# Second aggregation of a graph network: one exp per edge weight, and the sum of weights partly formed on VectorE

## The chip, the cores and the metric

One core of one Trainium2 chip runs the whole program in one launch. The metric is the device time of that launch in microseconds (us), lower is better.

## The reference, cut to what matters

Two graph attention networks follow each other on 1250 nodes and 21250 edges (20000 given, and one loop per node). The change lies in the first layer of the second network: 4 heads of 512 channels each. For a head with node scores a_s (source) and a_d (destination):

```
e(s, d)  = leaky_relu(a_s[s] + a_d[d], 0.2)            for every edge s -> d
p(s, d)  = exp(e(s, d) - max over the edges into d)
out[d]   = sum over s of p(s, d) * h[s]  /  (sum over s of p(s, d) + 1e-16)  + b
h        = elu(out)
```

## The kernel before, in words

The kernel treats the graph as a dense matrix: CT[s, d] counts the edges from s to d (125 rows of sources by 10 tiles of sources by 1250 destinations). Its last stages are `project_layer1`, which computes h and the scores, `aggregate_layer1` (L1489), which is the formula above, `project_out_layer1` and `aggregate_last`. Stages are separated by a barrier of all engines.

`aggregate_layer1` runs over 4 heads, per head over 3 pieces of the destinations (418, 416 and 416 columns, called thirds), per third over 10 tiles of 125 sources: 12 thirds, 120 steps. In the code g is the step, n the third (`ENDS` is 12), s the source tile, i the head.

In one step ScalarE (`act`) computes two exponentials of a 125x416 tile, since leaky_relu(x) is max(x, 0.2x): exp(u + a) and exp(v + 0.2a), where u and v are rows that depend on the destination and a is the score of the source, a column of one value per partition (`col_src`, L1641). VectorE (`dve`) takes the larger of the two (L1696), bounds it by 1 and multiplies it with CT (L1698). That is the weight p. ScalarE rounds p to the format that TensorE takes (`p_hi`, L1611), VectorE subtracts to get the rest (`p_lo`, L1688). TensorE (`pe`) then runs 14 products of 416 columns: for each of the four chunks of 128 channels three (h_hi p_hi, h_hi p_lo, h_lo p_hi; L1755), and two of p_hi and p_lo with a matrix of ones (L1735), which give the sum of the weights, the same in all 128 rows. They stand ahead of the step's other products, in step 0 behind them.

A third fills five banks of PSUM: four chunks and the sums. There are eight, so the next third reuses banks: its chunk 3 needs the bank of chunk 0 of the third before (`bank_is_free`, waiting for `left`), its sums that of chunk 1.

The end of a third is done inside the next third, at hand-placed steps. At s = 3 VectorE copies the sums out of PSUM (`invert`, L1665), takes the reciprocal (L1667) and multiplies chunks 0 and 1 by it (`leave`, L1676), at s = 4 chunks 2 and 3. ScalarE does the exponential of the elu for one chunk in each of s = 4 to 7, three instructions each (`elu_exp`, L1623, L1625, L1627), and VectorE finishes one chunk in each of s = 6 to 9 (`elu`, L1683). SyncE (`sp`) stores each finished chunk.

Every engine takes its instructions in the order of the code. In step g ScalarE issues the two exponentials of g and then rounds p of g-1; VectorE issues maximum and product of g and then the rest of p of g-1. Buffers of e, p_hi and p_lo go round in a ring of six (`RING`), so ScalarE's rounding of step g waits until TensorE has used step g-6 (`p_used`).

`col_src` is written once, in `project_layer1` (`spread_scores`, L1367 and L1368).

Of the kernel before, what the change touches and what calls it, by code (L numbers as in the profile page):

```python
# [4 lines left out]
F32 = mybir.dt.float32  # L5
F32R = mybir.dt.float32r
# [4 lines left out]
ALU = mybir.AluOpType  # L11
ACT = mybir.ActivationFunctionType
# [5 lines left out]
T = 125  # L18
NT = N // T
# [1133 lines left out]
def project_layer1(nc, core, xT, x2_rows, w, wa, h_rows, score_rows, col_src, u_col, v_col):  # L1153
# [13 lines left out]
    with ExitStack() as ctx:  # L1167
# [182 lines left out]
        def _(dve):  # L1350
# [13 lines left out]

            def spread_scores():
                dve.wait_ge(score_kept, NT)
                v.tensor_copy(col_src[0][:, 0:heads, :], score[:, 0])  # L1367
                v.tensor_scalar(col_src[1][:, 0:heads, :], score[:, 0], SLOPE, None, ALU.mult)  # L1368

            def maximum(m):  # L1370
# [118 lines left out]
def aggregate_layer1(nc, core, h_rows, col_src, bias, turned_rows, w_next):  # L1489


    CT = core.CT
    THIRDS = [(0, 418), (418, 416), (834, 416)]
    W = THIRD
# [2 lines left out]
    STEPS_ALL = H1 * STEPS  # L1497
    ENDS = 3 * H1
    RING = 6
    PER = CW + 1  # L1500
    with ExitStack() as ctx:
        sb, pb, sem = core.tools(ctx)
        uv_other = sb("uv", [T, 2, N], F32)
        uv = (first_uv_of_layer1(core), uv_other[:])
        h = sb("h_parts", [T, NT, 2, C1], F32)
        e = sb("e", [T, RING, 2, W], F32)
        p_hi = sb("p_hi", [T, RING, W], F32R)
        p_lo = sb("p_lo", [T, RING, W], F32R)
        ones_f = sb("ones_f", [T, 128], F32)
# [9 lines left out]
        bias_in = sem("bias_in")  # L1519
        ones_set = sem("ones_set")  # L1520
        exp_ready = sem("exp_ready")
        more_ready = sem("more_ready")
        p_ready = sem("p_ready")
        p_hi_ready = sem("p_hi_ready")
        p_split = sem("p_split")
# [18 lines left out]
        def bank(n, c):  # L1544
            return (n * PER + c) % 8

# [9 lines left out]
        @block.sync  # L1556
        def _(sp):
            def load_third(i, t3):
                a, w = THIRDS[t3]
                if i >= 2:  # L1560
                    sp.wait_ge(exp_ready, (i - 2) * STEPS + (t3 + 1) * NT)
                for kind in range(2):
                    dma_in_two(sp, uv[i % 2][:, kind, a:a + w],
                               core.uv_rows[kind, i * NT:(i + 1) * NT, :].rearrange("(o t) p -> o (t p)", o=1)[:, a:a + w]
                               .broadcast_to([T, w]), uv_in[i % 2][t3])

            def load_h(i, s):
                if i:
                    sp.wait_ge(p_used, (i - 1) * STEPS + 2 * NT + s + 1)
                dma_in_two(sp, h[:, s], h_rows[i, s * T:(s + 1) * T], h_loaded[s])  # L1570

            def store(n, c):
                i, t3 = divmod(n, 3)
                a, w = THIRDS[t3]
                sp.wait_ge(out_ready, n * CW + c + 1)
                sp.dma_start(turned_rows[i * CW + c, :, a:a + w], out_f[:, n % 2, c, 0:w]).then_inc(stored[n % 2][c], 16)

            sp.dma_start(b_col[:], bias).then_inc(bias_in, 16)
            for stored_h in core.h1_stored:
                sp.wait_ge(stored_h, 64 * (UNITS - 1))  # L1580
            for s in range(NT):
                load_h(0, s)
            for n in range(ENDS):
                i, t3 = divmod(n, 3)
                if i + 1 < H1:
                    load_third(i + 1, t3)
                stores = [c for c in range(CW) if n]
                if n == ENDS - 4:
                    sp.wait_ge(core.h1_stored[1], 64 * UNITS)
                    sp.wait_ge(core.h1_late, 64)  # L1590
                for s in range(NT):
                    if t3 == 2 and i + 1 < H1:
                        load_h(i + 1, s)
                    if s >= 2 and stores:
                        store(n - 1, stores.pop(0))
            sp.dma_start(core.w_first[:], w_next[0].rearrange("(k p) c -> p k c", p=128)[:, 0:K1 // 2, :]).then_inc(core.w_first_in, 16)
            for s in range(2):
                for c in range(CW):
                    sp.wait_ge(stored[s][c], 16 * (ENDS // 4))
            for t in range(2):  # L1600
                sp.dma_start(core.f_raw[:, t], turned_rows[0:K1 // 2, :, t * T:(t + 1) * T].rearrange("k p n -> p k n")).then_inc(core.f_first_in, 16)

        @block.scalar
        def _(act):
            a = nc.scalar
            def round_p(g):
                w = THIRDS[g // NT % 3][1]
                act.wait_ge(p_ready, g + 1)
                if g >= RING:
                    act.wait_ge(p_used, g - RING + 1)  # L1610
                a.activation(p_hi[:, g % RING, 0:w], e[:, g % RING, 0, 0:w], ACT.Copy).then_inc(p_hi_ready, 1)  # L1611

            def elu_exp(n, c):
                i, t3 = divmod(n, 3)
# [14 lines left out]
            for g in range(STEPS_ALL):  # L1629
                n, s = divmod(g, NT)  # L1630
                i, t3 = divmod(n, 3)
                at, w = THIRDS[t3]
                if s == 0:
                    if i == 0:
                        act.wait_ge(core.first_uv_in, 64)
                    else:
                        act.wait_ge(uv_in[i % 2][t3], 64 * ((i + 1) // 2))
                if g >= RING:
                    act.wait_ge(p_split, g - RING + 1)
                for kind in range(2):  # L1640
                    last = a.activation(e[:, g % RING, kind, 0:w], uv[i % 2][:, kind, at:at + w], ACT.Exp,  # L1641
                                        bias=col_src[kind][:, i, s:s + 1])
                last.then_inc(exp_ready, 1)
                if g == 0:
                    act.wait_ge(ones_set, 1)
                    a.activation(ones[:], ones_f[:], ACT.Copy).then_inc(ones_set, 1)
                if g:
                    round_p(g - 1)
                if g == 3:
                    act.wait_ge(bias_in, 16)  # L1650
                    a.activation(b_minus[:], b_col[:], ACT.Copy, scale=-1.0).then_inc(bias_in, 16)
                    act.wait_ge(bias_in, 32)
                if n and 4 <= s < 8:
                    elu_exp(n - 1, s - 4)
            round_p(STEPS_ALL - 1)

        @block.vector
        def _(dve):
# [2 lines left out]

            def invert(n):
                w = THIRDS[n % 3][1]
                dve.wait_ge(summed, n + 1)
                v.tensor_scalar(sums[:, 0, 0:w], p_o[:, bank(n, CW), 0:w], 1e-16, None, ALU.add).then_inc(sum_kept, 1)  # L1665
                dve.wait_ge(sum_kept, n + 1)
                v.reciprocal(sums[:, 1, 0:w], sums[:, 0, 0:w]).then_inc(inverted, 1)  # L1667
                dve.wait_ge(inverted, n + 1)
# [16 lines left out]
            def rest_of_p(g):  # L1685
                w = THIRDS[g // NT % 3][1]
                dve.wait_ge(p_hi_ready, g + 1)
                v.tensor_tensor(p_lo[:, g % RING, 0:w], e[:, g % RING, 0, 0:w], p_hi[:, g % RING, 0:w].bitcast(F32),  # L1688
                                ALU.subtract).then_inc(p_split, 1)

            for g in range(STEPS_ALL):
                n, s = divmod(g, NT)
                at, w = THIRDS[n % 3]
                low = e[:, g % RING, 0, 0:w]
                dve.wait_ge(exp_ready, g + 1)
                v.tensor_tensor(low, low, e[:, g % RING, 1, 0:w], ALU.max).then_inc(more_ready, 1)  # L1696
                dve.wait_ge(more_ready, g + 1)
                v.scalar_tensor_tensor(low, low, 1.0, CT[:, s, at:at + w], ALU.min, ALU.mult).then_inc(p_ready, 1)  # L1698
                if g:
                    rest_of_p(g - 1)  # L1700
                if n and s == 3:
                    invert(n - 1)
                    leave(n - 1, 0)
                    leave(n - 1, 1)
                if n and s == 4:
                    leave(n - 1, 2)
                    leave(n - 1, 3)
                if n and 6 <= s:
                    elu(n - 1, s - 6)
# [6 lines left out]
        def _(pe):  # L1716
# [10 lines left out]
                        pe.wait_ge(sum_kept, m + 1)  # L1727

            def sum_weights(g, n, s, w):
                if g == 0:  # L1730
                    pe.wait_ge(ones_set, 2)
                if s == 0:
                    bank_is_free(n, CW)
                for pp in (p_hi, p_lo):
                    last = nc.tensor.matmul(p_o[:, bank(n, CW), 0:w], ones[:], pp[:, g % RING, 0:w],  # L1735
                                            start=(s == 0 and pp is p_hi), stop=(s == NT - 1 and pp is p_lo))
                if s == NT - 1:
                    last.then_inc(summed, 1)
                return last

            for g in range(STEPS_ALL):
                n, s = divmod(g, NT)
# [2 lines left out]
                if t3 == 0:  # L1745
                    pe.wait_ge(h_loaded[s], 32 * (i + 1))
                pe.wait_ge(p_split, g + 1)
                if s:
                    sum_weights(g, n, s, w)
                for c in range(CW):  # L1750
                    if s == 0:
# [4 lines left out]
                                                start=(s == 0 and j == 0), stop=(s == NT - 1 and j == 2))  # L1756
                    if s == NT - 1 and c < CW - 1:
                        last.then_inc(chunk_done, 1)
                if s == 0:
                    last = sum_weights(g, n, s, w)  # L1760
                last.then_inc(p_used, 1)
            pe.wait_ge(left, (ENDS - 1) * CW)
            keep_busy(nc, core.ident, p_o[:, bank(ENDS - 2, CW - 1), 0:128], 14)
# [917 lines left out]
```

## Time and profile before

| | us |
|---|---|
| median of 3 runs | 1923.69 (1923.25 to 1928.69) |
| the profiled execution, its own time | 1930.16 |
| its span, first to last instruction | 1928.4 |
| TensorE busy / VectorE busy / ScalarE busy | 1839.7 / 1443.6 / 1030.9 |
| `aggregate_layer1`: first product to last | 1273.6 to 1609.5 |

The profile shows one execution. Durations are of single instructions; since an engine can start an instruction while the one before it finishes, the distance from start to start can be shorter than a duration. A time in square brackets at the end of a timeline row is the idle time of the engine before it, and what ended it. Matmuls are pipelined, so their durations overlap by about half.

### The profile page before, as it was taken

What the parts mean: (1) busy time and instruction counts of PE and PEld (TensorE: products, weight loads), DVE (VectorE), ACT (ScalarE), POOL (GpSimd) and SP (SyncE); (2) the same over time, 40 slices, a digit from 0 to 9 for tenths busy, and PEclk for the clock granted to TensorE, in tenths of its full rate; (3) what the DMA queues carried; (4) which work ended last, traced back from release to release, by engine and by line L of the source; (5) the groups of instructions that cost most, each with busy time, mean ns of one, the idle gap of its engine ahead of it and who ended that gap; (6) DMA issues with size and microseconds to landing.
All of it is one profiled execution on the core that took longest, in us unless ns stands there. A gap on an engine that the chain in (4) does not pass through costs nothing. (4 is left out here: it accounts for less than half of the span.)

```text
span 1928.4 us, 30682 instructions
## 1 busy us (share of the span) xinstructions
PE 1839.7 (95%) x11399; PEld 1776.6 (92%) x11399; DVE 1443.6 (75%) x2468; ACT 1030.9 (53%) x1634; POOL 142.1 (7%) x139
## 2 busy tenths in 40 slices
PE   7999999998999999998999999989999998999998
PEld 5877699998999999988999999989999998999997
DVE  8888599998888988965465549457888886346766
ACT  4676412218898889864211322257778875232632
POOL 5100211201000000000111011100000000000000
PEclk9999999999999999999999999989999999999989
DMA  4221335355455436619644466462342406544302
GB/s 126 67 64 54 99 103 149 101 133 142 134 111 131 108 77 149 145 16 248 185 141 143 135 208 188 141 193 79 108 143 66 138 28 204 156 129 126 99 9 80
DMA packets 179273, 234.12 MB, mean 121 GB/s; under 512 B 75943, under 2 KB 151655, under 8 KB 178889
## 3 DMA queue, kind: packets, MB, share of 16 engines
q1 hardware_dynamic: 170407, 202.98, 38.5%
q0 software_dynamic: 7984, 27.24, 4.9%
q10 hardware_dynamic: 748, 2.10, 0.4%
q8 instruction: 86, 1.41, 0.3%
q14 instruction: 48, 0.39, 0.1%
HBM read 167.27 MB, written 65.00 MB: 120 GB/s over the span
## 5 line engine op out<-in xcount | busy, mean ns | idle before, releaser
L1755 PE MATMUL p_o<-p_hi,h_parts 125*128 125x416 f32 (+1 forms) x960 | 283.0, 356 | 7.4 <-DVE z L1676 6.1
L1138 PE MATMUL p_o<-first_room,p 125*125 125x193 f32 x1200 | 202.2, 329 | 6.2 <-ACT res L1020 2.9
L1138 PEld LDWEIGHTS p_o<-first_room,p 125*125 125x125 f32 x1200 | 197.1, 189 | 8.0 <-issue 6.7
L1138 PE MATMUL p_o<-h_in,p 125*125 125x193 f32 x1200 | 200.9, 330 | 3.6 <-ACT res L1020 3.6
L1138 PEld LDWEIGHTS p_o<-h_in,p 125*125 125x125 f32 x1200 | 198.7, 190 | 5.0 <-issue 3.8
L1755 PEld LDWEIGHTS p_o<-p_hi,h_parts 125*128 125x128 f32 x960 | 182.0, 190 | 13.7 <-DVE z L1676 10.1
L781 DVE CUSTOM_DVE_ANT_0 max_junk<-src_row,G 125x1250 bf16<-125x1250 f32 x120 | 184.8, 1612 | 3.6 <-ACT src_row L819 1.5
L885 PE MATMUL p_h<-pw_hi,x1T 128*125 128x384 f32 x720 | 187.3, 341 | 0.0
L1088 DVE TENSOR_TENSOR e<-e 125x1250 f32<-125x1250 f32 x120 | 174.3, 1453 | 17.2 <-ACT e L1050 17.1
L1474 PE MATMUL p_h<-pw_hi,x2T 128*125 128x256 f32 (+1 forms) x960 | 177.8, 287 | 3.9 <-DVE h_out L1430 3.9
L1093 DVE SCALAR_TENSOR_TENSOR p<-e,CT 125x1250 f32<-125x1250 f32 x120 | 175.3, 1461 | 5.7 <-PE p_o L1138 1.7
L1755 PE MATMUL p_o<-p_lo,h_parts 125*128 125x416 f32 (+1 forms) x480 | 169.9, 354 | 0.0
L1050 ACT ACTIVATE e<-first_room,col 125x1250 f32<-125x1250 f32 x120 | 151.1, 1344 | 6.9 <-DVE p L1093 5.5
L1474 PEld LDWEIGHTS p_h<-pw_hi,x2T 128*125 128x125 f32 x960 | 150.4, 190 | 4.2 <-DVE h_out L1430 4.1
L1050 ACT ACTIVATE e<-uv,col 125x1250 f32<-125x1250 f32 x120 | 149.0, 1349 | 1.2 <-DVE p L1093 1.2
L1474 PE MATMUL p_h<-pw_lo,x2T 128*125 128x256 f32 (+1 forms) x480 | 136.9, 285 | 0.0
L885 PEld LDWEIGHTS p_h<-pw_hi,x1T 128*125 128x125 f32 x720 | 131.7, 188 | 1.2 <-issue 1.2
L2012 PE MATMUL p_y<-fw_hi,f_hi 128*125 128x384 f32 x360 | 121.9, 339 | 4.2 <-DVE fw_lo L1935 4.1
L885 PE MATMUL p_h<-pw_lo,x1T 128*125 128x384 f32 x360 | 122.5, 340 | 0.0
L2012 PE MATMUL p_y<-fw_lo,f_hi 128*125 128x384 f32 x360 | 121.6, 338 | 0.0
L2012 PE MATMUL p_y<-fw_hi,f_lo 128*125 128x384 f32 x360 | 121.5, 337 | 0.0
L481 PE MATMUL p_count<-src_hot,dst_hot 125*125 125x416 bf16 (+1 forms) x588 | 112.7, 350 | 6.3 <-DVE dst_hot L286 6.3
(285 smaller groups left out, 3839.3 us busy)
## 6 DMA issues: line engine op xcount, KB each, us to landing
f_raw<-turned SPq DMA_DIRECT2D x40, 500.0 KB, 8.8
h_parts<-h_rows SPq DMA_DIRECT2D x40, 448.0 KB
turned<-tail_room SPq DMA_DIRECT2D x18, 625.0 KB, 6.9
G<-turned SPq DMA_DIRECT2D x20, 562.5 KB
h_rows<-tail_room SPq DMA_DIRECT2D x22, 424.4 KB
h_rows<-h_out SPq DMA_DIRECT2D x16, 560.0 KB
h_rows<-tail_room SPq DMA_DIRECT2D x14, 560.0 KB
first_room<-in_w_gat POOLq DMA_DIRECT2D x36, 192.0 KB, 2.7
```

The lines of the kernel that those rows point to most:

```text
L481: last = nc.tensor.matmul(p_count[:, i, 0:w], dst_hot[:, h, :], src_hot[:, h, a:a + w], start=False, stop=False, skip_group_check=True)
L781: v.tensor_tensor_reduce(out=junk[:, t % 2, :], in0=src_row[:, h % 2, :], in1=G[:, t, :], scale=1.0, scalar=NO_EDGE, op0=ALU.subtract, op1 ...
L885: last = nc.tensor.matmul(p_h[:, (u * NT + t) % 4, 0:width], xp[:, k, at], wp[:, u, k, :], start=(k == 0 and n == 0), stop=(k == KD - 1 an ...
L1050: last = a.activation(e[:, g % RING, kind, :], uv[hh][:, kind, :], ACT.Exp, bias=col_src[kind][:, bass.ds(i * 2 + hh, 1), s])
L1088: v.tensor_tensor(e[:, g % RING, 0, :], e[:, g % RING, 0, :], e[:, g % RING, 1, :], ALU.max).then_inc(more_ready, 1)
L1093: v.scalar_tensor_tensor(p[:, g % RING, :], e[:, g % RING, 0, :], 1.0, CT[:, s, :], ALU.min, ALU.mult).then_inc(p_ready, 1)
L1138: last = nc.tensor.matmul(p_o[:, b, n * 256:n * 256 + C0 + 1], p[:, g % RING, d * T:(d + 1) * T], h_in[hh][:, s, 0:C0 + 1], start=(s == 0 ...
L1474: last = nc.tensor.matmul(p_h[:, n % 4, 0:width], xp[:, k, at], wp[:, q % 2, k, 0:width], start=(k == 0 and j == 0), stop=(k == KD - 1 and ...
L1755: last = nc.tensor.matmul(p_o[:, bank(n, c), 0:w], h[:, s, kind, cols].bitcast(F32R), pp[:, g % RING, 0:w], start=(s == 0 and j == 0), sto ...
L2012: last = nc.tensor.matmul(p_y[:, t % 2, half, 0:CW], fp[:, n % 2, kk, :], wp[:, k, cols], start=(k == 0 and j == 0), stop=(k == KO - 1 and ...
```

## The change

Three things, all in `aggregate_layer1`, and one line in `project_layer1`.

1. Since exp is monotone, the larger is taken first: VectorE computes max(u + 0.8a, v) in one instruction two steps ahead (`larger_exponent`, `AHEAD` = 2), and ScalarE takes one exp of it, with 0.2a as bias. `col_src[0]` now holds 0.8a.
2. The weights of source tiles 0 to 3 are added on VectorE (`add`, three instructions per third), the sum is rounded (`acc_hi`, ScalarE) and its rest taken (`acc_lo`, VectorE), and TensorE multiplies these two with ones in step 6 instead of the eight products with ones of steps 0 to 3.
3. The copy of the sums out of PSUM moves from VectorE to ScalarE (`keep_sums`), which issues it in s = 3 behind the rounding.

```
 def spread_scores():
-    v.tensor_copy(col_src[0][:, 0:heads, :], score[:, 0])
+    v.tensor_scalar(col_src[0][:, 0:heads, :], score[:, 0], 1 - SLOPE, None, ALU.mult)

 # load_third (SyncE)
-    sp.wait_ge(exp_ready, (i - 2) * STEPS + (t3 + 1) * NT)
+    sp.wait_ge(larger, (i - 2) * STEPS + (t3 + 1) * NT)

 # ScalarE
+def keep_sums(n):
+    act.wait_ge(summed, n + 1)
+    if n:
+        act.wait_ge(inverted, n)
+    a.activation(sums[:, 0, 0:w], p_o[:, bank(n, CW), 0:w], ACT.Copy, bias=1e-16).then_inc(sum_kept, 1)
 for g in range(STEPS_ALL):
-    if g >= RING:
-        act.wait_ge(p_split, g - RING + 1)
-    for kind in range(2):
-        last = a.activation(e[:, g % RING, kind, 0:w], uv[i % 2][:, kind, at:at + w], ACT.Exp,
-                            bias=col_src[kind][:, i, s:s + 1])
-    last.then_inc(exp_ready, 1)
+    act.wait_ge(larger, g + 1)
+    a.activation(e[:, g % RING, 0:w], e[:, g % RING, 0:w], ACT.Exp, bias=col_src[1][:, i, s:s + 1]).then_inc(exp_ready, 1)
     if g:
         round_p(g - 1)
+    if s == ADDED:
+        act.wait_ge(added, (n + 1) * (ADDED - 1))
+        if n:
+            act.wait_ge(p_used, (n - 1) * NT + SUM_AT + 1)
+        a.activation(acc_hi[:, 0:w], acc[:, 0:w], ACT.Copy).then_inc(acc_hi_ready, 1)
+    if n and s == 3:
+        keep_sums(n - 1)
     if n and 4 <= s < 8:
         elu_exp(n - 1, s - 4)
 round_p(STEPS_ALL - 1)
+keep_sums(ENDS - 1)

 # VectorE
 def invert(n):
-    dve.wait_ge(summed, n + 1)
-    v.tensor_scalar(sums[:, 0, 0:w], p_o[:, bank(n, CW), 0:w], 1e-16, None, ALU.add).then_inc(sum_kept, 1)
     dve.wait_ge(sum_kept, n + 1)
     v.reciprocal(sums[:, 1, 0:w], sums[:, 0, 0:w]).then_inc(inverted, 1)
+def larger_exponent(g):
+    if s == 0:
...
+    if g >= RING:
+        dve.wait_ge(p_split, g - RING + 1)
+    v.scalar_tensor_tensor(e[:, g % RING, 0:w], uv[i % 2][:, 0, at:at + w], col_src[0][:, i, s:s + 1],
+                           uv[i % 2][:, 1, at:at + w], ALU.add, ALU.max).then_inc(larger, 1)
+def add(g):
...
+    dve.wait_ge(p_ready, g + 1)
+    v.tensor_tensor(acc[:, 0:w], before, e[:, g % RING, 0:w], ALU.add).then_inc(added, 1)
+def rest_of_sum(n):
+    dve.wait_ge(acc_hi_ready, n + 1)
+    v.tensor_tensor(acc_lo[:, 0:w], acc[:, 0:w], acc_hi[:, 0:w].bitcast(F32), ALU.subtract).then_inc(acc_split, 1)
+for g in range(AHEAD):
+    larger_exponent(g)
 for g in range(STEPS_ALL):
     dve.wait_ge(exp_ready, g + 1)
-    v.tensor_tensor(low, low, e[:, g % RING, 1, 0:w], ALU.max).then_inc(more_ready, 1)
-    dve.wait_ge(more_ready, g + 1)
     v.scalar_tensor_tensor(low, low, 1.0, CT[:, s, at:at + w], ALU.min, ALU.mult).then_inc(p_ready, 1)
+    if g + AHEAD < STEPS_ALL:
+        larger_exponent(g + AHEAD)
     if g:
         rest_of_p(g - 1)
+    if 0 < s < ADDED:
+        add(g)
+    if s == ADDED + 1:
+        rest_of_sum(n)
     if n and s == 3:
         invert(n - 1)
         leave(n - 1, 0)

 # TensorE
 def sum_weights(g, n, s, w):
-    if s == 0:
+    if s == ADDED:
         bank_is_free(n, CW)
+    passing = [p_hi[:, g % RING, 0:w], p_lo[:, g % RING, 0:w]]
+    if s == SUM_AT:
+        pe.wait_ge(acc_split, n + 1)
+        passing += [acc_hi[:, 0:w], acc_lo[:, 0:w]]
+    for k, pp in enumerate(passing):
+        last = nc.tensor.matmul(p_o[:, bank(n, CW), 0:w], ones[:], pp,
+                                start=(s == ADDED and k == 0), stop=(s == NT - 1 and k == 1))
...
-    if s:
+    if s >= ADDED:
         sum_weights(g, n, s, w)
...
-    if s == 0:
-        last = sum_weights(g, n, s, w)
```

`ADDED` is 4 and `SUM_AT` is 6. The ring of e holds one tile per step instead of two.

## Rows read from the trace of the kernel before

**Rows 1.** Busy time by stretch: window, length, PE, PEld, DVE, ACT, POOL, clock, DMA.

```profile
1385.00:1413.00 28.00, 27.44 (x144) 26.78 (x143) 24.28 (x42) 22.79 (x44) 0.00 (x0) 1.00 0.15 48
```

**Rows 2.** Who waited for whom, 1270 to 1625: us in total, times, longest.

```profile
ACT tail_room L1623 <- DVE z L1676: 45.2, 11, 6.5
DVE e L1696 <- ACT e L1641: 39.2, 39, 1.4
...
PEld p_o L1755 <- DVE z L1676: 10.1, 11, 1.0
DVE sums L1665 <- PE p_o L1735: 9.9, 2, 5.4
```

**Rows 3.** Timeline of VectorE in one third: start, duration, line, operation, idle before.

```profile
1388.32 2.77 DVE L1667 RECIPROCAL sums<-sums 128x418 f32<-128x418 f32 x1
...
1404.31 0.59 DVE L1696 TENSOR_TENSOR e<-e 125x416 f32<-125x416 f32 x1 [0.93 <-ACT e L1641]
1404.94 0.59 DVE L1698 SCALAR_TENSOR_TENSOR e<-e,CT 125x416 f32<-125x416 f32 x1
1405.45 0.58 DVE L1688 TENSOR_TENSOR p_lo<-e,p_hi 125x416 fp32r<-125x416 f32 x1
1405.95 0.65 DVE L1683 SCALAR_TENSOR_TENSOR tail_room<-z,b_col,tail_room 128x418 f32<-128x418 f32 x1
1406.52 0.58 DVE L1696 TENSOR_TENSOR e<-e 125x416 f32<-125x416 f32 x1
...
1415.85 2.75 DVE L1667 RECIPROCAL sums<-sums 128x416 f32<-128x416 f32 x1
```

**Rows 4.** Timeline of ScalarE in the same third.

```profile
1391.75 0.65 ACT L1623 ACTIVATE tail_room<-z,b_minus 128x418 f32<-128x418 f32 x1 [3.88 <-DVE z L1676]
...
1393.47 1.16 ACT L1641 ACTIVATE e<-uv,col 125x416 f32<-125x416 f32 x2
1394.54 0.54 ACT L1611 ACTIVATE p_hi<-e 125x416 fp32r<-125x416 f32 x1
1394.98 0.63 ACT L1623 ACTIVATE tail_room<-z,b_minus 128x418 f32<-128x418 f32 x1
```

**Rows 5.** Timeline of TensorE in the same third.

```profile
1384.00 0.35 PE L1735 MATMUL p_o<-p_hi,ones 125*128 125x418 f32 x1
...
1386.67 0.35 PE L1735 MATMUL p_o<-p_hi,ones 125*128 125x418 f32 x1
...
1391.77 0.46 PE L1755 MATMUL p_o<-p_hi,h_parts 125*128 125x416 f32 x1 [0.56 <-DVE z L1676]
```

**Rows 6.** Groups of VectorE by line and shape: busy us, mean ns, idle before.

```profile
L1698 DVE SCALAR_TENSOR_TENSOR e<-e,CT 125x416 f32<-125x416 f32 x80 | 47.4, 593 | 2.8
...
L1688 DVE TENSOR_TENSOR p_lo<-e,p_hi 125x416 fp32r<-125x416 f32 x80 | 46.9, 586 | 1.2 <-ACT p_hi L1611 1.2
...
L1683 DVE SCALAR_TENSOR_TENSOR tail_room<-z,b_col,tail_room 128x416 f32<-128x416 f32 x28 | 18.1, 646 | 0.0
```

**Rows 7.** ScalarE's copy of 384 columns out of PSUM, in another stage.

```profile
L846 ACT ACTIVATE tail_room<-p_h x60: 491/493/497, 245.4 to 431.9; 125x384 f32<-125x384 f32 x60
```

**Rows 8.** VectorE timeline: the first reciprocal, the last two, the start of the next stage.

```profile
1305.71 2.77 DVE L1667 RECIPROCAL sums<-sums 128x418 f32<-128x418 f32 x1
...
1581.06 2.75 DVE L1667 RECIPROCAL sums<-sums 128x416 f32<-128x416 f32 x1
...
1607.42 0.59 DVE L1665 TENSOR_SCALAR sums<-p_o 128x416 f32<-128x416 f32 x1 [5.42 <-PE p_o L1735]
1608.05 2.75 DVE L1667 RECIPROCAL sums<-sums 128x416 f32<-128x416 f32 x1
...
1613.87 0.18 DVE L2185 CAST fw_hi<-wa 128x32 fp32r<-128x32 f32 x1 [0.94 <-PEq L70]
```

**Rows 9.** TensorE timeline: the product behind the first third's wait for h.

```profile
1280.43 0.71 PE L1735 MATMUL p_o<-p_hi,ones 125*128 125x418 f32 x1 [3.85 <-DMA h_parts<-h_rows]
```

**Rows 10.** The small instruction of `spread_scores`.

```profile
L1367 DVE COPY col<-score x1: 174/174/174, 1111.4 to 1111.4; 125x40 f32<-125x40 f32 x1
```

More of the change, by code:

```diff
@@ L1499, in aggregate_layer1 @@
     RING = 6
+    AHEAD = 2
+    ADDED = 4
+    SUM_AT = ADDED + 2
     PER = CW + 1
@@ L1505, in aggregate_layer1 @@
         h = sb("h_parts", [T, NT, 2, C1], F32)
-        e = sb("e", [T, RING, 2, W], F32)
+        e = sb("e", [T, RING, W], F32)
+        acc = sb("acc", [T, W], F32)
+        acc_hi = sb("acc_hi", [T, W], F32R)
+        acc_lo = sb("acc_lo", [T, W], F32R)
         p_hi = sb("p_hi", [T, RING, W], F32R)
@@ L1521, in aggregate_layer1 @@
         exp_ready = sem("exp_ready")
-        more_ready = sem("more_ready")
+        larger = sem("larger")
+        added = sem("added")
+        acc_hi_ready = sem("acc_hi_ready")
+        acc_split = sem("acc_split")
         p_ready = sem("p_ready")
@@ L1610, in round_p @@
                     act.wait_ge(p_used, g - RING + 1)
-                a.activation(p_hi[:, g % RING, 0:w], e[:, g % RING, 0, 0:w], ACT.Copy).then_inc(p_hi_ready, 1)
+                a.activation(p_hi[:, g % RING, 0:w], e[:, g % RING, 0:w], ACT.Copy).then_inc(p_hi_ready, 1)
+            def keep_sums(n):
+                w = THIRDS[n % 3][1]
+                act.wait_ge(summed, n + 1)
+                if n:
+                    act.wait_ge(inverted, n)
+                a.activation(sums[:, 0, 0:w], p_o[:, bank(n, CW), 0:w], ACT.Copy, bias=1e-16).then_inc(sum_kept, 1)
             def elu_exp(n, c):
@@ L1632, in _ @@
                 at, w = THIRDS[t3]
-                if s == 0:
[L1634 to L1637, printed above, removed]
-                if g >= RING:
-                    act.wait_ge(p_split, g - RING + 1)
-                for kind in range(2):
-                    last = a.activation(e[:, g % RING, kind, 0:w], uv[i % 2][:, kind, at:at + w], ACT.Exp,
-                                        bias=col_src[kind][:, i, s:s + 1])
-                last.then_inc(exp_ready, 1)
+                act.wait_ge(larger, g + 1)
+                a.activation(e[:, g % RING, 0:w], e[:, g % RING, 0:w], ACT.Exp, bias=col_src[1][:, i, s:s + 1]).then_inc(exp_ready, 1)
                 if g == 0:
@@ L1687, in rest_of_p @@
                 dve.wait_ge(p_hi_ready, g + 1)
-                v.tensor_tensor(p_lo[:, g % RING, 0:w], e[:, g % RING, 0, 0:w], p_hi[:, g % RING, 0:w].bitcast(F32),
+                v.tensor_tensor(p_lo[:, g % RING, 0:w], e[:, g % RING, 0:w], p_hi[:, g % RING, 0:w].bitcast(F32),
                                 ALU.subtract).then_inc(p_split, 1)
+            def larger_exponent(g):
+                n, s = divmod(g, NT)
+                i, t3 = divmod(n, 3)
+                at, w = THIRDS[t3]
+                if s == 0:
+                    if i == 0:
+                        dve.wait_ge(core.first_uv_in, 64)
+                    else:
+                        dve.wait_ge(uv_in[i % 2][t3], 64 * ((i + 1) // 2))
+                if g >= RING:
[3 more added lines that the diff above has]
+            def add(g):
+                n, s = divmod(g, NT)
+                w = THIRDS[n % 3][1]
+                if s == 1:
+                    if n:
+                        dve.wait_ge(acc_split, n)
+                    before = e[:, (g - 1) % RING, 0:w]
+                else:
+                    dve.wait_ge(added, n * (ADDED - 1) + s - 1)
+                    before = acc[:, 0:w]
+                dve.wait_ge(p_ready, g + 1)
+                v.tensor_tensor(acc[:, 0:w], before, e[:, g % RING, 0:w], ALU.add).then_inc(added, 1)
+            def rest_of_sum(n):
+                w = THIRDS[n % 3][1]
+                dve.wait_ge(acc_hi_ready, n + 1)
+                v.tensor_tensor(acc_lo[:, 0:w], acc[:, 0:w], acc_hi[:, 0:w].bitcast(F32), ALU.subtract).then_inc(acc_split, 1)
+            for g in range(AHEAD):
+                larger_exponent(g)
             for g in range(STEPS_ALL):
@@ L1693, in _ @@
                 at, w = THIRDS[n % 3]
-                low = e[:, g % RING, 0, 0:w]
+                low = e[:, g % RING, 0:w]
                 dve.wait_ge(exp_ready, g + 1)
-                v.tensor_tensor(low, low, e[:, g % RING, 1, 0:w], ALU.max).then_inc(more_ready, 1)
-                dve.wait_ge(more_ready, g + 1)
                 v.scalar_tensor_tensor(low, low, 1.0, CT[:, s, at:at + w], ALU.min, ALU.mult).then_inc(p_ready, 1)
+                if g + AHEAD < STEPS_ALL:
+                    larger_exponent(g + AHEAD)
                 if g:
                     rest_of_p(g - 1)
+                if 0 < s < ADDED:
+                    add(g)
+                if s == ADDED + 1:
+                    rest_of_sum(n)
                 if n and s == 3:
@@ L1729, in sum_weights @@
             def sum_weights(g, n, s, w):
-                if g == 0:
+                if g == ADDED:
                     pe.wait_ge(ones_set, 2)
-                if s == 0:
+                if s == ADDED:
                     bank_is_free(n, CW)
-                for pp in (p_hi, p_lo):
-                    last = nc.tensor.matmul(p_o[:, bank(n, CW), 0:w], ones[:], pp[:, g % RING, 0:w],
-                                            start=(s == 0 and pp is p_hi), stop=(s == NT - 1 and pp is p_lo))
+                passing = [p_hi[:, g % RING, 0:w], p_lo[:, g % RING, 0:w]]
[5 more added lines that the diff above has]
+                                            start=(s == ADDED and k == 0), stop=(s == NT - 1 and k == 1))
                 if s == NT - 1:
                     last.then_inc(summed, 1)
-                return last
             for g in range(STEPS_ALL):
@@ L1758, in _ @@
                         last.then_inc(chunk_done, 1)
-                if s == 0:
-                    last = sum_weights(g, n, s, w)
                 last.then_inc(p_used, 1)
```

## The prediction

> **What bounds the kernel now.** I read the busy times by stretch first, then the waits, then the timelines of VectorE, ScalarE and TensorE over one third. In 28 us in the middle of the stage TensorE is busy for 27.44, VectorE for 24.28, ScalarE for 22.79, at full clock [rows 1]. By the busy shares alone TensorE would be the bound. The waits say otherwise: in 12 thirds VectorE waits for TensorE only twice, and for ScalarE's exponentials 39 times, 39.2 us in all; TensorE waits once in each of eleven thirds for z, the chunk that VectorE must take out before its bank is free, 10.1 us in all [rows 2]. An engine that nobody waits for in the steady thirds, and that itself waits once in each, has slack. TensorE's slot is (1386.67 - 1384.00) / 14 = 0.1907 us per product [rows 5], so its 140 products of a third take 26.7 us. The third takes (1581.06 - 1305.71) / 10 = 27.54 us, reciprocal to reciprocal [rows 8].
>
> What makes 27.54 is a chain through VectorE and ScalarE, and it closes from rows. From the reciprocal at 1388.32, z of chunk 0 is there when ScalarE starts the elu at 1391.75, 3.43 us later [rows 3, 4]. ScalarE then has, in order, four elus of 1.72 (1391.75 to 1393.47), and between them three times a pair of exps (1.07) and a rounding (0.44) [rows 4]: 6.86 + 4.53. Behind the fourth elu it gives the exp pair of step 8, 1.16 long, and VectorE, idle until then, starts 0.03 later. Sum 3.43 + 6.86 + 4.53 + 1.19 = 16.01; the row stands at 1404.31 - 1388.32 = 15.99 [rows 3]. From there VectorE never idles: steps 8 and 9 and steps 0 to 3 of the next third at 0.63 + 0.51 + 0.50 = 1.64 from start to start, two elus of 0.57, and the copy of the sums, 0.62: 9.8 + 1.1 + 0.6 = 11.5, against 1415.85 - 1404.31 = 11.54 [rows 3]. Total 27.53.
>
> **The change, part by part.**
>
> One exp instead of two. ScalarE's pair of 1.07 becomes one of 0.53, 0.63 long (half the pair's slot, and 1.16 less that) [rows 4]. Four of them lie in the chain: 2.12 us per third come off it. The other six lie where ScalarE waits for VectorE, and bring nothing.
>
> The larger taken first. The maximum (0.63 from start to start, because the product behind it needs its result) goes, and an addition and maximum with a column operand comes. It has a twin in the trace: the elu's last instruction, the same two operations with a column, 646 ns long, 0.57 from start to start, against 0.51 for the product without a column [rows 3, 6]. It depends on nothing just ahead of it, being two steps early. A step on VectorE is then 0.51 + 0.56 + 0.505 = 1.575, 0.06 less than before. What the trace does not show is one such instruction right behind the product. Its start is bounded from below by the 0.51 that any independent successor gets, from above by the 0.63 of a dependent one [rows 3]. I take 0.51, since it is independent, and keep 0.63 for a rival. ScalarE waits for it, but step g's is issued one full step ahead of its use.
>
> The sum of four tiles. VectorE gets three additions and one subtraction per third, 0.505 each from start to start (the slot between 1405.45 and 1405.95, same form) [rows 3]. The additions stand in steps 1 to 3, inside the chain: +1.52. The subtraction stands in step 5, where VectorE goes on to wait for ScalarE's exp: covered. ScalarE's rounding of the sum, 0.54 like the other rounding, stands at s = 4 ahead of the first elu, where ScalarE sits idle for 3.88 us during the reciprocal [rows 4]; were that cover gone it would add 0.45.
>
> TensorE loses eight products with ones and gets two: 6 fewer per third, 134 x 0.1907 = 25.55 us. It waits for the rest of the sum in step 6, many microseconds after step 5 on VectorE. I expect no stall.
>
> The copy of the sums on ScalarE. VectorE's 0.62 leaves the chain. ScalarE takes some 0.52: 384 columns take 493 ns [rows 7], and 32 more at most 0.03 more; below, nothing reasonable under 0.49. Behind its wait for TensorE are queued exp 4, the rounding of 3, the rounding of the sum and the first elu, about 1.4 us of work that fits in the reciprocal's 2.8. It is a new hop, TensorE to ScalarE to VectorE, worth 0.03 as the other hops.
>
> Nothing changes for the queues of SyncE and GpSimd: no DMA is added or moved, and the one wait of SyncE that is renamed comes true earlier. The multiplication in `spread_scores` replaces a 0.17 us copy in another stage, where it is one of hundreds of small instructions [rows 10]: nothing.
>
> **The sum for a steady third.** 3.43 + 6.86 + 3 x (0.53 + 0.44) + 0.63 + 0.03 = 13.86 to the start of step 8's product; then six steps of 1.575, two elus of 0.565 and three additions of 0.505: 9.45 + 1.13 + 1.52 = 12.10. Total 25.96, 1.58 less. Can TensorE follow? From the reciprocal its chunk 3 begins 3.45 later [rows 3, 5]; up to the end of step 9's ones there are 3 + 36 + 70 + 2 + 2 = 113 products, 112 x 0.1907 + 0.35 for the last, 0.04 to wake ScalarE, 0.52 + 0.03 for the copy: 25.75. The same sum with 119 products gives 26.34 for the last third of before, where the row shows 1607.42 - 1581.06 = 26.36 [rows 8]. So TensorE's loop is 0.2 shorter than the other, which keeps the say.
>
> The ends. In the first third TensorE sets the pace and waits for h to land, until 1280.43 [rows 9]; what it saves before that is lost. Behind it are four fewer products up to the sums: 0.8. In the last third VectorE waits for TensorE (5.42) [rows 8]: six fewer products, 1.1. The stage ends with the same reciprocal and four multiplications, and the next begins at the barrier [rows 8], so its work moves forward whole.
>
> Together 10 x 1.58 + 0.8 + 1.1 = 17.7 us. The profiled execution took 1930.16 at a span of 1928.4; it would give 1912.5 at 1910.7. It lies 6.5 above the median of 1923.69, in work the change does not touch, so the median becomes **1906.0**.
>
> **The rivals.**
>
> TensorE sets the pace (0.13). If one of ScalarE's or VectorE's slots is a little shorter than I take it, the third falls to the 25.75 of TensorE's loop: 17.9 + 1.9, 1903.9. For it speaks that only 0.2 us lie between the loops; against it, that the same slots reproduced 27.54 to 0.01.
>
> The instruction with a column does not overlap with the product ahead of it (0.12). Then 0.11 more in each of six steps of the chain, 26.6: 9.2 + 1.9, 1912.6. No pair of this form stands in the trace.
>
> VectorE becomes the bound outright, and the kernel slower (0.03). The place is the start of each VectorE instruction: today it begins 0.08 before the one ahead ends (0.50 between starts at 0.58 long) [rows 3]. If in the new order, where every instruction carries a wait and an increment for another engine, they ran end to end, a third would be 10 x (0.593 + 0.646 + 0.586) + 8 x 0.586 + 4 x 0.646 + 2.75 = 28.3 [rows 6, 3]. This is 0.8 above 27.54, ten times, less 1.9: 1929.4. It turns slower than before once a third passes 27.7, that is 1.8 above my sum. Against it: the subtraction at 1405.45 and the elu behind it carry both and overlap. The Trainium skill (VectorE: DVE Perf Modes, Terms) says that each VectorE instruction is followed by a drain and the next cannot issue until the pipe is empty; by that rule this case would be the likely one. The trace does not agree, with 0.50 between the starts of instructions of 0.58.
>
> Something behind the stage gives part back (0.04). The following stage's first inputs are loaded by SyncE during the last third; if they came late, a few microseconds would return, 1910 or so. Both the stores ahead of them and the stage's end move forward together, so I see no reason.
>
> **How the numbers follow.** The forecast has 0.68. Its own uncertainty is 0.3 us per third, 3 us in all, and the runs of before reach 5.0 above their median, which gives 1902.5 to 1911.5; this takes in the first rival and stops just short of the second. A measurement tells about 0.3% (5.8 us) from nothing. Faster by more, below 1917.9: the forecast, both close rivals, and most of the rest, 0.94. Within: 0.03, a mixture of the last two. Slower: 0.03.
>
> **What would show it right or wrong.** Reciprocals 25.96 apart (25.75 and no idle of VectorE ahead of the products if TensorE leads; 26.6 if the column instruction is dear); the new instruction's mean near 646 ns and 0.56 to its successor; VectorE waiting for exps in steps 7 and 8 only, about 0.5 each; VectorE's reciprocal following the last addition with no idle; 1608 products in place of 1680, and TensorE's wait for z down from about 0.9 to 0.4 per third. I am wrong in the mechanism if TensorE waits for `p_lo` within a third, or if the third shrinks by something other than the exps.

## The result, and the profile after

The changed kernel takes 1907.91 us (median of 4 runs, 1905.64 to 1911.14) against 1925.05 for the kernel before beside it (4 runs), a ratio of 0.9909 with a 95% interval of 0.9891 to 0.9927: about 17 us less. The forecast was 1906.0 from 1923.69, 17.7 less. A second measurement, with the experiments, gave 0.9921 (0.9907 to 0.9934), about 15 us less. One execution of an experiment took 4993.24 us and one of the kernel before, beside it, 6732.26: the figures below leave both out.

The profiled execution has a span of 1903.9 us. That is 24.5 less than the profiled one of before, more than the medians show, and the stages say where the rest lies. Taken from TensorE's first instruction of `aggregate_layer1` to VectorE's first of the next stage, the stage fell by 19.76 us (345.22 to 325.46); what is ahead of it took 3.84 less in this execution and what follows 0.90 less. Behind the stage the change touches nothing, and ahead of it only the small instruction of [rows 10]; over the fourteen profiled executions of this study the stage began anywhere from 1263.16 to 1271.65, whatever the kernel.

The busy times by stretch of the changed kernel, the same 28 us as in [rows 1], with the same columns:

```profile
1385.00:1413.00 28.00, 27.81 (x148) 27.18 (x147) 27.04 (x48) 20.27 (x39) 0.00 (x0) 1.00 0.28 81
```

Here the reader sees the exchange: VectorE went from 24.28 to 27.04 of 28, ScalarE from 22.79 to 20.27, and TensorE runs 148 products where it ran 144.

Who waited for whom in the changed kernel, 1270 to 1600 (us in total, times, longest), answering to [rows 2]:

```profile
ACT sums L1629 <- PE p_o L1793: 36.6, 12, 8.6
ACT p_hi L1622 <- DVE e L1746: 33.0, 44, 0.9
ACT tail_room L1641 <- DVE z L1691: 23.6, 11, 2.2
DVE sums L1682 <- ACT sums L1629: 12.7, 2, 8.2
DVE e L1746 <- ACT e L1652: 10.1, 22, 0.5
...
PEld p_o L1812 <- DVE z L1691: 5.5, 11, 0.6
```

VectorE's waits for exps went from 39, 39.2 us in all, to 22 of about 0.46 each, two per third. TensorE's waits for z halved, 10.1 to 5.5. VectorE waits for the sums only twice, in the first third and the last: ahead of the ten reciprocals between it never waits, so TensorE still does not lead.

The timeline of VectorE over one third, from reciprocal to reciprocal, answering to [rows 3]:

```profile
1377.47 2.76 DVE L1682 RECIPROCAL sums<-sums 128x418 f32<-128x418 f32 x1
...
1388.64 0.59 DVE L1746 SCALAR_TENSOR_TENSOR e<-e,CT 125x416 f32<-125x416 f32 x1 [0.46 <-ACT e L1652]
1389.15 0.65 DVE L1717 SCALAR_TENSOR_TENSOR e<-uv,col 125x416 f32<-125x416 f32 x1
1389.72 0.58 DVE L1703 TENSOR_TENSOR p_lo<-e,p_hi 125x416 fp32r<-125x416 f32 x1
1390.22 0.64 DVE L1698 SCALAR_TENSOR_TENSOR tail_room<-z,b_col,tail_room 128x418 f32<-128x418 f32 x1
...
1391.33 0.59 DVE L1746 SCALAR_TENSOR_TENSOR e<-e,CT 125x416 f32<-125x416 f32 x1 [0.47 <-ACT e L1652]
...
1402.87 0.58 DVE L1732 TENSOR_TENSOR acc<-acc,e 125x416 f32<-125x416 f32 x1
1403.37 2.75 DVE L1682 RECIPROCAL sums<-sums 128x416 f32<-128x416 f32 x1
```

A third takes 1403.37 - 1377.47 = 25.90 us. The new instruction (L1717) is 0.65 long, and its successor starts 0.57 after it; it starts itself 0.51 after the product ahead of it (L1746). VectorE idles in steps 7 and 8 only, and the reciprocal follows the last addition without a gap.

The timeline of ScalarE in the same third, answering to [rows 4]:

```profile
1376.90 0.52 ACT L1629 ACTIVATE sums<-p_o 128x418 f32<-128x418 f32 x1 [2.40 <-PE p_o L1793]
1377.32 0.63 ACT L1652 ACTIVATE e<-e,col 125x416 f32<-125x416 f32 x1
1377.85 0.54 ACT L1622 ACTIVATE p_hi<-e 125x416 fp32r<-125x416 f32 x1
1378.30 0.54 ACT L1666 ACTIVATE acc_hi<-acc 125x416 fp32r<-125x416 f32 x1
1380.89 0.65 ACT L1641 ACTIVATE tail_room<-z,b_minus 128x418 f32<-128x418 f32 x1 [2.06 <-DVE z L1691]
...
1382.62 0.63 ACT L1652 ACTIVATE e<-e,col 125x416 f32<-125x416 f32 x1
1383.15 0.54 ACT L1622 ACTIVATE p_hi<-e 125x416 fp32r<-125x416 f32 x1
1383.59 0.63 ACT L1641 ACTIVATE tail_room<-z,b_minus 128x418 f32<-128x418 f32 x1
```

The first elu begins 3.42 after the reciprocal, as before. Between two elus stand an exp of 0.53 and a rounding of 0.44, where a pair of 1.07 stood. The copy out of PSUM takes 0.52 and ends 0.05 ahead of VectorE's reciprocal here (1377.47): that is how little TensorE's loop is ahead in this third. One third later it ends 0.15 ahead. All that is queued behind it is done 2.06 us before the elu can begin.

The reciprocals at the ends, and the next stage's first instruction, answering to [rows 8]:

```profile
1299.78 2.77 DVE L1682 RECIPROCAL sums<-sums 128x418 f32<-128x418 f32 x1 [4.53 <-ACT sums L1629]
...
1558.75 2.74 DVE L1682 RECIPROCAL sums<-sums 128x416 f32<-128x416 f32 x1
...
1584.45 2.75 DVE L1682 RECIPROCAL sums<-sums 128x416 f32<-128x416 f32 x1 [8.16 <-ACT sums L1629]
...
1590.27 0.18 DVE L2240 CAST fw_hi<-wa 128x32 fp32r<-128x32 f32 x1 [0.95 <-PEq L70]
```

Ten thirds take 258.97 where they took 275.35: 16.38 us. The last one fell from 26.99 to 25.70, 1.29. The end of the stage is 5.82 behind its last reciprocal, before and after, so all of it is passed on.

### The profile page after: what moved, and what is told of

It is laid out like the page before. It is cut to its first block and busy times, and to the rows that moved or that the text cites. A ratio compares the mean times of both kernels' runs of the same rounds, so it can differ in the third digit from the quotient of the medians.

```text
span 1903.9 us, 30552 instructions
## 1 busy us (share of the span) xinstructions
PE 1818.4 (96%) x11327; PEld 1757.4 (92%) x11327; DVE 1456.4 (76%) x2504; ACT 981.2 (52%) x1538; POOL 140.9 (7%) x139
## 5 line engine op out<-in xcount | busy, mean ns | idle before, releaser
L1812 PE MATMUL p_o<-p_hi,h_parts 125*128 125x416 f32 (+1 forms) x960 | 277.5, 356 | 6.9 <-DMA h_parts<-h_rows 5.2
```

Source lines behind the costliest of these rows:

```text
L1812: last = nc.tensor.matmul(p_o[:, bank(n, c), 0:w], h[:, s, kind, cols].bitcast(F32R), pp[:, g % RING, 0:w], start=(s == 0 and j == 0), sto ...
```

## The experiments

Theory: two loops close once per third, that is, each leads from one reciprocal back to the next, and the longer sets the time of the third. One goes through VectorE and ScalarE (reciprocal, z, four elus with exps between them, then VectorE's work up to the next reciprocal): 27.54 before, 25.90 after. The other goes through TensorE (z, the products up to the sums, their copy, the reciprocal): about 26.9 before, 25.75 after. Rivals: TensorE alone sets the pace, by its products; or VectorE and ScalarE do, whatever TensorE has to do. The third is read from the profile, as a tenth of the time between the first reciprocal and the eleventh; a ratio is to the kernel before, with its 95% interval.

**The sum of four tiles alone**, on the kernel before:

```diff
+                if 0 < s < ADDED:
+                    add(g)
+                if s == ADDED + 1:
+                    rest_of_sum(n)
...
-                if s:
+                if s >= ADDED:
                     sum_weights(g, n, s, w)
```

> The kernel before with only the sum of four source tiles moved to VectorE (two exps per weight, copy of the sums on VectorE); ones_f lies in the room of z. Theory (the loop of VectorE and ScalarE sets the pace): three additions of 0.505 us come into the loop, a third goes from 27.54 to 29.05 us, the kernel is about 13 us slower than before although TensorE has 72 products less. Rival (TensorE sets the pace): a third falls by 6 x 0.19 to 26.4, the kernel is about 13 us faster.

Measured: 1941.93 us, ratio 1.0085 (1.0063 to 1.0108), slower by some 16 us by the ratio, 15 by the medians. VectorE's timeline:

```profile
1305.77 2.77 DVE L1680 RECIPROCAL sums<-sums 128x418 f32<-128x418 f32 x1
...
1596.19 2.75 DVE L1680 RECIPROCAL sums<-sums 128x416 f32<-128x416 f32 x1
```

The waits of that kernel, 1270 to 1630:

```profile
PEld p_o L1793 <- DVE z L1689: 29.0, 11, 3.6
```

TensorE's timeline around two of these waits, and the 5 us behind each of them (the columns of [rows 1]):

```profile
1367.29 0.46 PE L1793 MATMUL p_o<-p_hi,h_parts 125*128 125x418 f32 x1 [1.72 <-DVE z L1689]
...
1396.35 0.46 PE L1793 MATMUL p_o<-p_hi,h_parts 125*128 125x416 f32 x1 [3.28 <-DVE z L1689]
```

```profile
1367.29:1372.29 5.00, 5.00 (x26) 4.94 (x27) 4.93 (x10) 4.87 (x10) 0.00 (x0) 1.00 0.20 73
```

```profile
1396.35:1401.35 5.00, 5.00 (x18) 4.81 (x19) 4.93 (x10) 4.87 (x10) 0.00 (x0) 0.66 0.00 0
```

A third is 29.04 us. TensorE has the same 72 products less as in the full change, and its waits for z grew from 10.1 us to 29.0. They alternate between 1.7 and 3.3 us, and behind the wait of 3.28 TensorE's granted clock was 0.66 of full speed over 5 us, where it was 1.00 behind the wait of 1.72; the thirds are 29.02 to 29.06 long all the same. TensorE's load did not set the time of the kernel before. This part of the change is a loss by itself: it adds three instructions to the loop that leads.

**One exp alone** (the changed kernel with sum and copy put back):

```diff
-                for k, pp in enumerate(passing):
+                for pp in (p_hi, p_lo):
...
+                v.tensor_scalar(sums[:, 0, 0:w], p_o[:, bank(n, CW), 0:w], 1e-16, None, ALU.add).then_inc(sum_kept, 1)
```

> The changed kernel with the sum of weights and the copy of the sums put back as before: one exp per weight alone. Theory: the loop of VectorE and ScalarE falls to 25.90 - 1.51 + 0.62 = 25.0, so that TensorE's loop of 119 products between two reciprocals takes over: 3.45 + 22.5 + 0.39 + 0.62 = 26.96 per third, about 6 us faster than before. Rival (TensorE's load is of no account, VectorE and ScalarE set the pace throughout): 25.0 per third, about 25 us faster.

Measured: 1919.07 us, ratio 0.9971 (0.9958 to 0.9983). VectorE's timeline, the second row being its copy of the sums:

```profile
1307.31 2.77 DVE L1676 RECIPROCAL sums<-sums 128x418 f32<-128x418 f32 x1
...
1333.61 0.59 DVE L1674 TENSOR_SCALAR sums<-p_o 128x416 f32<-128x416 f32 x1 [1.80 <-PE p_o L1779]
...
1576.92 2.75 DVE L1676 RECIPROCAL sums<-sums 128x416 f32<-128x416 f32 x1
```

26.96 per third. By the sum of the expectation the loop of VectorE and ScalarE is down to 25.0, 2.5 us less, but only 0.57 arrives, since TensorE's loop is next: VectorE now waits 1.8 to 2.0 for the sums in each of the ten thirds. The rival's 25.0 per third, 25 us in all, did not come.

**The copy on ScalarE alone**, on the kernel before:

```diff
-                v.tensor_scalar(sums[:, 0, 0:w], p_o[:, bank(n, CW), 0:w], 1e-16, None, ALU.add).then_inc(sum_kept, 1)
...
+                if n and s == 3:
+                    keep_sums(n - 1)
```

> The kernel before with only the copy of the sums moved to ScalarE. Theory: 0.62 us leave the loop of VectorE and ScalarE, 27.54 to 26.9 per third, which is also TensorE's loop (26.9): about 6 us faster than before. Rival (the copy lay in a wait for TensorE and cost nothing): 27.5, no difference.

Measured: 1918.94 us, ratio 0.9969 (0.9951 to 0.9988), 26.94 per third.

```profile
1300.70 2.77 DVE L1675 RECIPROCAL sums<-sums 128x418 f32<-128x418 f32 x1 [5.04 <-ACT sums L1618]
...
1570.14 2.75 DVE L1675 RECIPROCAL sums<-sums 128x416 f32<-128x416 f32 x1
```

One small instruction, moved, is worth as much alone as the 120 exps alone, but for another reason. Here VectorE does not wait for the sums between the first third and the last: the 0.59 is nearly the whole 0.62 of the copy. ScalarE's copy ends only 0.03 to 0.05 ahead of each reciprocal, so that the two loops are equal as nearly as this run can tell.

**One exp and the copy, without the sum:**

```diff
-                if s >= ADDED:
+                if s:
                     sum_weights(g, n, s, w)
```

> The changed kernel with only the sum of weights put back on TensorE (140 products per third). Theory: the loop of VectorE and ScalarE is down to 24.4, TensorE's loop sets the pace: 3.45 + 22.5 + 0.39 + 0.55 = 26.9 per third, 6.5 us faster than before and some 11 slower than the changed kernel; VectorE waits for the sums in every third. Rival (the additions on VectorE cost more than the products they save): 24.4 per third, faster than the changed kernel.

Measured: 1919.42 us, ratio 0.9963 (0.9947 to 0.998). VectorE's timeline, and the waits of this kernel, 1270 to 1630:

```profile
1300.84 2.77 DVE L1677 RECIPROCAL sums<-sums 128x418 f32<-128x418 f32 x1 [5.03 <-ACT sums L1629]
...
1569.70 2.75 DVE L1677 RECIPROCAL sums<-sums 128x416 f32<-128x416 f32 x1 [2.36 <-ACT sums L1629]
```

```profile
DVE sums L1677 <- ACT sums L1629: 38.3, 12, 9.2
```

26.89 per third, and now VectorE waits for the sums in all twelve. Here TensorE leads, and the rival's 24.4 did not come. From this kernel to the changed one the sum of four tiles brings 0.99 us per third; on the kernel before the same edit cost 1.51.

**The copy back on VectorE**, in the changed kernel:

```diff
-                if n and s == 3:
-                    keep_sums(n - 1)
...
+                v.tensor_scalar(sums[:, 0, 0:w], p_o[:, bank(n, CW), 0:w], 1e-16, None, ALU.add).then_inc(sum_kept, 1)
```

> The changed kernel with only the copy of the sums put back on VectorE. Theory: 0.62 us come into the loop of VectorE and ScalarE, 25.90 to 26.5 per third, 6 us slower than the changed kernel. Rival (TensorE's loop sets the pace, which gets 0.07 longer): 25.97, under 1 us.

Measured: 1914.86 us, ratio 0.995 (0.9931 to 0.9969).

```profile
1297.23 2.77 DVE L1681 RECIPROCAL sums<-sums 128x418 f32<-128x418 f32 x1
...
1562.53 2.75 DVE L1681 RECIPROCAL sums<-sums 128x416 f32<-128x416 f32 x1
```

26.53 per third, 0.63 more than the changed kernel; the rival's 25.97 did not come. In that kernel, too, the loop of VectorE and ScalarE is the longer.

**Three tiles instead of four:**

```diff
-    ADDED = 4
+    ADDED = 3
```

> The changed kernel with the weights of three source tiles added on VectorE instead of four (136 products per third). Theory: VectorE's loop falls to 25.4, TensorE's rises by 2 x 0.19 to 26.1 and takes over: 26.1 per third, 2 us slower than the changed kernel, VectorE waiting for the sums in every third. Rival (TensorE has more slack than its loop says): 25.4 per third, 5 us faster.

Measured: 1913.01 us, ratio 0.9939 (0.9917 to 0.996).

```profile
1304.66 2.77 DVE L1682 RECIPROCAL sums<-sums 128x418 f32<-128x418 f32 x1 [5.03 <-ACT sums L1629]
...
1566.13 2.75 DVE L1682 RECIPROCAL sums<-sums 128x416 f32<-128x416 f32 x1 [0.63 <-ACT sums L1629]
```

26.15 per third. With two products more per third VectorE waits 0.63 for the sums: TensorE's loop has taken over. Four is where the loops nearly meet.

**The cover and the chain.** One more copy of 416 columns on ScalarE in the changed kernel, its result unused, once in step 4 ahead of the first elu, once in step 5 ahead of the second:

```diff
+                if n and s == 4:
+                    a.activation(spare[:, 0:w], CT[:, s, at:at + w], ACT.Copy)
```

(The other kernel has `s == 5` in the first line.)

> The changed kernel with one more copy of 416 columns on ScalarE in step 4, ahead of the first elu. Theory (this place is covered by VectorE's reciprocal, so that the rounding of the sum costs nothing there): 25.9 per third, no change. Rival: 26.35.

> The changed kernel with the same copy one step later, in step 5, between the first and the second elu. Theory (ScalarE's elus are part of the loop that sets the third): 0.45 us more, 26.35 per third, 4.5 us in all. Rival (TensorE or VectorE alone sets the third): 25.9, no change.

Measured, one run each, so that only the thirds can tell: 1908.28 and 1912.26 us. VectorE's timelines, step 4 and then step 5:

```profile
1300.44 2.77 DVE L1685 RECIPROCAL sums<-sums 128x418 f32<-128x418 f32 x1 [4.54 <-ACT sums L1630]
...
1559.39 2.74 DVE L1685 RECIPROCAL sums<-sums 128x416 f32<-128x416 f32 x1
```

```profile
1301.97 2.77 DVE L1685 RECIPROCAL sums<-sums 128x418 f32<-128x418 f32 x1 [4.54 <-ACT sums L1630]
...
1565.32 2.74 DVE L1685 RECIPROCAL sums<-sums 128x416 f32<-128x416 f32 x1
```

Ten thirds take 258.95 with the copy in step 4 and 263.35 in step 5, against 258.97. The same instruction costs nothing in one place and 0.44 us each time one step later. ScalarE is busy for less than three quarters of the stretch in the changed kernel (20.27 of 28), and is in the chain all the same.

**Each exp one step earlier**, so that the chain of elus no longer holds VectorE up:

```diff
-    AHEAD = 2
+    AHEAD = 3
...
+            def exp_of(g):
...
+            exp_of(0)
             for g in range(STEPS_ALL):
...
-                a.activation(e[:, g % RING, 0:w], e[:, g % RING, 0:w], ACT.Exp, bias=col_src[1][:, i, s:s + 1]).then_inc(exp_ready, 1)
...
                 if g:
                     round_p(g - 1)
+                if g + 1 < STEPS_ALL:
+                    exp_of(g + 1)
```

> The changed kernel with each exp issued one step earlier on ScalarE, behind the rounding, and the larger exponent three steps ahead instead of two. Theory: VectorE no longer waits for exps in steps 7 and 8 (2 x 0.47), its loop falls to 24.9 and TensorE's takes over: 25.75 per third, 1.5 us faster than the changed kernel. Rival (VectorE's waits for exps are covered by something else): 25.9.

Measured: 1907.18 us (the median of three runs), ratio 0.9913 (0.9878 to 0.9947), too wide to tell 1.5 us. The thirds tell it:

```profile
1302.44 2.77 DVE L1690 RECIPROCAL sums<-sums 128x418 f32<-128x418 f32 x1 [4.53 <-ACT sums L1629]
...
1560.23 2.75 DVE L1690 RECIPROCAL sums<-sums 128x416 f32<-128x416 f32 x1 [0.94 <-ACT sums L1629]
```

25.78 per third, and VectorE waits 0.94 for the sums (0.85 to 1.05 in the ten thirds): its own loop is now about 24.9, and TensorE's is 25.78.

**The same with five tiles added**, which uses that room:

```diff
-    ADDED = 4
+    ADDED = 5
```

> As exp_ahead, with the weights of five source tiles added on VectorE (132 products per third). Theory: TensorE's loop falls by 2 x 0.19 to 25.37, VectorE's is 25.4 with the fourth addition: 25.4 per third, 6 us faster than the changed kernel. Rival (the rounding of the sum, now between two elus, and the addition lengthen the loop of VectorE and ScalarE): 25.9 or more.

> The kernel with exps one step ahead and five tiles added, once more: 25.4 per third, 10 x 0.5 + 0.4 in the last third = 5 to 6 us below the changed kernel.

> The changed kernel once more, beside the next one on the same chip: 25.9 per third, some 17 us below the kernel before.

Measured: 1900.37 us, ratio 0.9872 (0.984 to 0.9904), and again, beside the changed kernel on one chip, 1902.87, ratio 0.9871 (0.9856 to 0.9886), against 0.9921 (0.9907 to 0.9934) for the changed kernel. The busy times over one of its thirds:

```profile
1307.00:1332.40 25.40, 25.35 (x135) 24.79 (x134) 25.36 (x45) 17.87 (x34) 0.00 (x0) 1.00 0.16 51
```

25.40 per third, and TensorE and VectorE are both busy for 25.35 of 25.40. It is faster than the kernel before and than the changed kernel. By the thirds it should gain over the changed kernel 5 us in ten and 0.4 in the last (25.31 for 25.71). In the profiled executions of this pair the stage is 6.52 us shorter: 5.09 in ten thirds, 0.40 in the last, 1.03 ahead of the first reciprocal (35.08 to 34.05). The medians show 9.4; the rest lies within what the intervals leave open, and I cannot place it.

## Why the prediction was right

**The bound.** I read the waits against the busy shares: TensorE busy for 27.44 of 28 was not the bound, because nobody waited for it. That held: taking 72 products off it, at the price of 48 instructions on VectorE, made the kernel slower by what those add to the other loop. But TensorE's loop was only some 0.6 us per third behind, and it is what cut short the gain of one exp alone.

**The sum for a third.** Predicted 25.96, measured 25.90. Its terms, predicted and in the rows above: to the first elu 3.43, 3.42; exp and rounding 0.97, 0.97; to the start of step 8's product 13.86, and 1391.33 - 1377.47 = 13.86; from there to the next reciprocal 12.10, and 1403.37 - 1391.33 = 12.04; the copy out of PSUM 0.52, 0.52. VectorE waits for exps in steps 7 and 8 and nowhere else, as forecast.

**The cover.** The rounding of the sum was put at nothing because ScalarE idles there, behind VectorE's reciprocal. The extra copy in step 4 cost nothing either; the same copy in step 5, outside that idle time, cost 0.44, which is what the cover is worth.

**TensorE's loop.** Predicted 25.75 and second by 0.2. The kernel with the exps ahead measures it at 25.78, so that it lies 0.12 behind the loop that leads. The rival that it sets the pace was close, but the two idles of VectorE and the missing gap ahead of the reciprocal speak against it, and the copy put back cost its whole 0.63.

**The column instruction.** The rival that it does not overlap with the product ahead fell with the first row: 0.51 from start to start. So did the slower case, instructions end to end: in the new order, too, VectorE's instructions start 0.50 to 0.57 apart at 0.58 to 0.65 long. The Trainium skill (VectorE: DVE Perf Modes, Terms) says that the next instruction cannot issue until the pipe of the one before is empty; as in the kernel before, the trace does not show them one behind the other.

**Behind the stage.** The rival that something there gives part back did not come: the next stage starts 5.82 behind the last reciprocal, as before.

**The ends.** Last third: 1.1 predicted, 1.29 measured. The prediction counted only the six products, though its own sum for TensorE's loop has the cheaper copy in it as well, which makes 1.2. First third: 0.8 predicted, and 2.09 measured in this pair of executions, 37.06 to 34.97 from TensorE's first instruction to the first reciprocal. Here the agreement of the totals is in part luck: over all fourteen profiled executions this stretch took 32.97 to 37.06 us, in the four kernels that keep all 140 products 33.05, 34.98, 35.66 and 37.06. A term of 0.8 cannot be told in that, and the one profile of the kernel before is the longest of all. The rows of the changed kernel that answer to [rows 9]:

```profile
1269.98 0.56 PE L1812 MATMUL p_o<-p_hi,h_parts 125*128 125x418 f32 x1 [2.93 <-DMA h_parts<-h_rows]
...
1276.35 0.46 PE L1812 MATMUL p_o<-p_hi,h_parts 125*128 125x418 f32 x1 [2.27 <-DMA h_parts<-h_rows]
```

TensorE's wait ahead of step 1 was 2.27 instead of 3.85 us; the last section says what that accounts for.

## What to carry to other kernels

Where two loops across engines close once per round, an engine that is busy for 98% need not set the pace: ask who waits for it. Add up each loop from starts in the timeline, not from busy times, and take for an edit the difference of the longer loop before and the longer loop after; its parts do not add up. Here one exp, the copy and the sum of four tiles, each alone, brought -0.57, -0.59 and +1.51 us per third, and together -1.64.

## What was not expected of the hardware

The first third spread by more than the change in it, and in the two executions compared below about half of the difference is TensorE's clock. Step 1 of the first third waits for h. The 5 us behind this wait, in the kernel before, in the changed kernel, and in the one with one exp and the copy but without the sum (columns as in [rows 1], with the share and GB/s of the DMA at the end):

```profile
1280.43:1285.43 5.00, 5.00 (x14) 4.78 (x15) 3.31 (x7) 1.73 (x4) 0.00 (x0) 0.50 1.03 265
```

```profile
1276.35:1281.35 5.00, 5.00 (x18) 4.83 (x19) 5.00 (x10) 2.69 (x5) 0.00 (x0) 0.66 1.05 259
```

```profile
1278.23 0.46 PE L1780 MATMUL p_o<-p_hi,ones 125*128 125x418 f32 x1 [0.86 <-DMA h_parts<-h_rows]
```

```profile
1278.23:1283.23 5.00, 5.00 (x26) 4.93 (x27) 5.00 (x10) 2.46 (x5) 0.00 (x0) 1.00 1.03 248
```

After 3.85 us without a product TensorE was granted half its clock (1.2 of 2.4 GHz) and ran 14 products in 5 us; after 2.27, 18 at a mean of 0.66; after 0.86, 26 at full clock. The waits for z in the kernel with the sum alone fit in with that, with far fewer transfers beside them: behind the 3.28 us 18 products at 0.66, behind the 1.72 us 26 at full clock. No run sets the length of such a wait on purpose, so that no more is shown than these five cases.

What it costs can be worked out. From the end of this wait to the first reciprocal took 25.28 us in the kernel before (to 1305.71), 23.43 in the changed one (to 1299.78) and 22.61 in the third (to 1300.84), which ran at full clock. The third has four products more than the changed kernel (0.76) and a copy that is 0.07 cheaper than in the kernel before. So the low clock cost about 25.28 - 22.61 - 0.07 = 2.6 us in the kernel before and 23.43 - 22.61 + 0.76 = 1.6 in the changed kernel: an estimate, from one execution of each. Of the 2.09 us between the two, 1.0 is the clock, 0.8 the four products and the copy, and 0.24 the landing of h (11.78 and 11.54 us behind the start of the stage). The ten thirds that follow repeat far better: 27.52 to 27.55 in the kernel before, 25.88 to 25.91 in the changed one.
